# Selective scan: the two halves of the weighted states are added on GpSimd ahead of its decay factors, and TensorE sums eight states in place of sixteen

## The reference, cut to what matters

```python
z = h @ in_w.T
gate = jax.nn.silu(h @ gate_w.T)
A = -jnp.exp(A_log)
Bi = z @ Bp_w.T
Ci = z @ Cp_w.T
dt = jax.nn.softplus(z @ dt_w.T + dt_b)
A_bar = 1.0 + dt[..., None] * A
def step(state, inp):
    a_bar, dtz_t, b_t, c_t = inp
    state = a_bar * state + dtz_t[:, :, None] * b_t[:, None, :]
    y = jnp.sum(state * c_t[:, None, :], axis=-1)    # over 16 states
    return (state, y)
...
y = jnp.swapaxes(ys, 0, 1) * gate
return y @ out_w.T
```

## Time and profile before

| | us |
|---|---|
| median of three runs | 2525.13 |
| the profiled execution | 2515.18 |
| its span, first to last instruction | 2513.4 |
| busy in the span: PE / DVE / ACT / POOL | 2233.5 / 1666.2 / 1317.3 / 809.1 |
| the scan, about | 824 to 953 of the span |
| two stretches of 13.40 us inside it (878.0 to 904.8), DVE busy in each | 11.99 |
| the same, PE and POOL busy in each | 13.40 and 5.96 |

### The profile page before, as it was taken

How to read it: one execution, slowest core, us unless ns; L and a number is a source line. 1 busy time by engine, 2 the same in 40 slices (tenths; PEclk the granted TensorE clock), 3 DMA queues, 4 the chain that set the end, 5 groups by cost and what they waited for, 6 DMA issues and landing times. The chain is left out here.

```text
span 2513.4 us, 48220 instructions
## 1 busy us (share of the span) xinstructions
PE 2233.5 (89%) x17198; PEld 1778.7 (71%) x17200; DVE 1666.2 (66%) x3232; ACT 1317.3 (52%) x3079; POOL 809.1 (32%) x1019
## 2 busy tenths in 40 slices
PE   6979798999698898989999879999689998899775
PEld 5857687887476796778888468888556566788652
DVE  5767635774575686764777456666567575888758
ACT  4558636664576653533666343333475464445345
POOL 4646502332354442100333112222110110544365
PEclk9989989999899899979999989999899999999888
DMA  3000081115200000060211420000200002777711
GB/s 112 2 1 2 32 331 64 51 51 175 92 2 2 22 2 1 2 259 20 101 51 51 175 103 1 2 1 1 101 1 1 1 1 77 227 212 212 231 28 34
DMA packets 102932, 178.35 MB, mean 71 GB/s; under 512 B 59687, under 2 KB 71591, under 8 KB 97578
## 3 DMA queue, kind: packets, MB, share of 16 engines
q1 hardware_dynamic: 85514, 135.93, 16.3%
q0 software_dynamic: 9792, 28.85, 3.6%
q10 hardware_dynamic: 7392, 10.49, 1.1%
HBM read 112.44 MB, written 62.78 MB: 70 GB/s over the span
## 5 line engine op out<-in xcount | busy, mean ns | idle before, releaser
L2289 POOL TENSOR_TENSOR l2a_Pn<-l2a_Pn,l2a_rden 128x1024 f32<-128x1024 f32 x32 | 60.1, 1899 | 295.2 <-DVE l2a_rden L2531 295.2
L1617 ACT ACTIVATE l0f_w_parts<-l0f_W 128x512 fp32r (+1 forms) x117 | 90.4, 775 | 68.2 <-PE l0f_psG L1422 50.3
L1768 DVE TENSOR_TENSOR l0f_w_parts<-l0f_W,l0f_w_parts 128x512 fp32r<-128x512 f32 (+1 forms) x117 | 99.2, 867 | 37.7 <-ACT l0f_w_parts L1617 37.6
L1617 ACT ACTIVATE l1f_w_parts<-l1f_W 128x512 fp32r (+1 forms) x117 | 90.4, 774 | 63.0 <-PE l1f_psG L1422 50.2
L4054 POOL TENSOR_TENSOR l3x_Pn<-l3x_Pn,l3x_fac 128x616 f32<-128x616 f32 (+2 forms) x96 | 70.4, 763 | 149.8 <-DVE l3x_fac L4133 140.4
L1768 DVE TENSOR_TENSOR l1f_w_parts<-l1f_W,l1f_w_parts 128x512 fp32r<-128x512 f32 (+1 forms) x117 | 99.2, 867 | 12.6 <-ACT l1f_w_parts L1617 12.2
L1475 PE MATMUL l1f_psY<-l1f_W,l1f_XT_hT 128*128 (+1 forms) x440 | 104.2, 380 | 0.8 <-ACT l1f_XT_hT L1597 0.8
L883 ACT ACTIVATE l1a_att_Pn<-l1a_att_psS,l1a_att_nmx 128x128 f32<-128x128 f32 x256 | 92.1, 422 | 1.7 <-DVE l1a_att_nmx L1002 1.7
L883 ACT ACTIVATE l0x_Pn<-l0x_psS,l0x_nmx 128x128 f32<-128x128 f32 x256 | 92.1, 422 | 0.9 <-DVE l0x_nmx L1002 0.9
L706 POOL TENSOR_TENSOR l1a_att_Pn<-l1a_att_Pn,l1a_att_rden 128x512 f32<-128x512 f32 x64 | 66.6, 1041 | 73.3 <-DVE l1a_att_rden L1009 73.3
L1475 PEld LDWEIGHTS l1f_psY<-l1f_W,l1f_XT_hT 128*128 128x128 f32 x440 | 80.3, 190 | 10.8 <-issue 1.0
(11 more groups left out here) (860 smaller groups left out, 7504.4 us busy)
## 6 DMA issues: line engine op xcount, KB each, us to landing
relative_rows<-l3x_ext SPq DMA_DIRECT2D x32, 516.0 KB, 5.8
l1f_W<-in_l1f_w SPq DMA_DIRECT2D x9, 1536.0 KB, 20.6
l0f_W<-in_l0f_w SPq DMA_DIRECT2D x8, 1536.0 KB, 26.1
cumulative_rows<-l3x_cum SPq DMA_DIRECT2D x32, 384.0 KB, 3.4
l3x_K<-keys SPq DMA_DIRECT2D x16, 512.0 KB, 5.5
l3x_rel<-relative_rows SPq DMA_DIRECT2D x32, 231.0 KB, 4.3
values<-l1f_W SPq DMA_DIRECT2D x11, 512.0 KB, 4.4
l3x_V<-values SPq DMA_DIRECT2D x16, 308.0 KB
```

Of the source, the lines that this page charges most:

```text
L1617: nc.scalar.activation(w_high[i], W[:, bass.ds(act_offsets[k] + o, m)], ACT.Copy).then_inc(high_ready, 1)
L1768: nc.vector.tensor_tensor(w_low[i], W[:, bass.ds(dve_offsets[k] + o, m)], w_high[i], ALU.subtract).then_inc(low_ready, 1)
L2289: nc.gpsimd.tensor_tensor(part, part, rden[b % 2][:, 8 * u:8 * u + 8].unsqueeze(2).to_broadcast([P, 8, P]), ALU.mult)\
```

## The change

GpSimd gets a new step `add_halves(p)`: u[:, 0:1024] = u[:, 0:1024] + u[:, 1024:2048], one 128x1024 f32 addition in SBUF. It waits for the second `weigh` of pair p and stands in GpSimd's list behind L1980 of pair p+1 and ahead of the decay factors of pair p+1 (for p = 7, at the list's end). `sum_states(p)` waits for it and takes eight blocks where it took sixteen.

```diff
+    halved = R.sem("states_halved")
...
+        def add_halves(p):
+            pool.wait_ge(weighted, 2 * p + 2)
+            nc.gpsimd.tensor_tensor(half(u[p % 2], 0), half(u[p % 2], 0), half(u[p % 2], 1), ALU.add).then_inc(halved, 1)
+
         for p in range(NP2):
             pool.wait_ge(xn_ready, p + 1)
             xp = G.x[:, 2 * p * D:2 * (p + 1) * D]
             nc.gpsimd.tensor_tensor(xp, xp, saved[:, 2 * p * D:2 * (p + 1) * D], ALU.add).then_inc(summed, 1)
+            if p:
+                add_halves(p - 1)
             pool.wait_ge(dt_ready, p + 1)
...
+        add_halves(NP2 - 1)
...
         def sum_states(p):
             past(pe, x_ready, 2 * p)
-            for s in range(ST):
-                if s % HS == 0:
-                    pe.wait_ge(weighted, 2 * p + s // HS + 1)
-                ins = nc.tensor.matmul(psS, G.ident[:, :], u[p % 2][:, s * P:(s + 1) * P], start=(s == 0), stop=(s == ST - 1))
+            pe.wait_ge(halved, p + 1)
+            for s in range(HS):
+                ins = nc.tensor.matmul(psS, G.ident[:, :], u[p % 2][:, s * P:(s + 1) * P], start=(s == 0), stop=(s == HS - 1))
             ins.then_inc(sum_done, 1)
```

## The result

| | before | after |
|---|---|---|
| median of six runs, us | 2524.16 (2518.23 to 2528.76) | 2534.87 (2530.99 to 2538.71) |
| ratio of the runs, 95% interval | 1 | 1.0047 (1.0034 to 1.0060) |
| span of the profiled execution, us | 2513.4 | 2533.6 |
| the scan: first `gates` reciprocal to the next sublayer's first VectorE instruction on x (L539), us | 118.73 | 127.96 |
| the rest of the span, us | 2394.7 | 2405.6 |

The change makes the kernel slower by 0.47% (0.34 to 0.60); the medians lie 10.7 us apart. The scan accounts for 9.2 us. The spans lie 20.2 us apart, and the other 11 us of that are in the main scatter of single traces. The scan begins 6.7 us later in the trace of the changed kernel (842.0 against 835.3 us), so that much was lost in sublayers that run before any edited instruction.

The account below looks back on a forecast made before the run. No engine fills the kernel alone; in the scan TensorE and VectorE are in turn on the path, GpSimd off it. 9.0 + 0.9 + 0.4 - 0.5 = +9.8 us on 2525.13 gives 2534.9 us, range 2519 to 2546.

Parts of the forecast that it names:

- pairs 2 to 6: Steady pairs of the scan: each 1.8 us longer, five times 1.8, +9.0 us.
- the end: Last pair's sum: starts later with half the blocks, 2.7 to 3.1 us long; `gate_y` released 0.5 us earlier (0 to -1.3).
- The addition: GpSimd's new 128x1024 f32 addition per pair: takes 2.36 us, bounds 1.90 to 2.52.
- Step 2: VectorE's dtz, with two SBUF inputs, stands behind GpSimd's addition, making VectorE about 2.08 us late per pair.
- Step 3: After the addition, dtz was waiting first and goes ahead of GpSimd's decay pass, 0.29 us.
- rival B: GpSimd keeps its turn, dtz also stands behind the first decay pass, 1.99 us more; +17.1, 2542 us; chance 0.10.
- Step 4: VectorE through `drive` keeps its pace; `gate_y` loses its 1.34 us wait; first scan ready 0.74 us later.
- Step 5: GpSimd's addition to x starts 0.1 us before the first scan is ready; the scan stands another 1.04 us.
- The sum does not wait for GpSimd: B products occupy TensorE until about 892.75, past the addition's end at 892.25; the sum runs 892.75 to 894.6.
- Rival A: The two engines don't hamper each other enough to matter; the wait goes: -10.4, 2514.7 us; chance 0.12.
- Rival C: TensorE's clock falls in its longer gaps; two such stretches cost 0.9 per pair, 5 to 6 us, 2540 us; chance 0.06.
- Rival D: Only dtz collides and the addition to x slips past the scans: +4.5, 2529.6 us; chance 0.12.

Follow-up runs that it names:

- e4: Changed kernel with GpSimd's addition cut from 1024 to 128 columns and seven of the second eight states left out of the sum; one run, 2516.98 us.
- e6: Changed kernel with a 128x2048 memset in place of GpSimd's addition, second eight states left out of the sum; one run, 2518.58 us.
- e9: Changed kernel with VectorE's dtz moved from behind dt to just before `drive`; one run, 2524.15 us.
- e2: Changed kernel with the addition written to a tile nobody reads and all sixteen blocks summed; ratio to before 1.0039 (1.0019 to 1.0058).
- e1: Kernel before with TensorE summing only states 0 to 7 and no addition on GpSimd; ratio to before 0.9956 (0.9939 to 0.9972).
- e10: The changed kernel once more, unaltered, for a second trace; ratio to before 1.0037 (1.0023 to 1.0052).
- e3: Changed kernel with GpSimd's addition to x waiting until both scans of the pair before are done; ratio to before 1.0014 (1.0003 to 1.0025).
- e5: Changed kernel with the next pair's dt and dtz taken between the two `weigh`s, before the event releasing the addition; ratio to before 1.0017 (1.0005 to 1.0030).
- e8: Changed kernel with e3's and e5's edits, ScalarE making decay factors 8 to 11, its copies first, VectorE adding the last halves; ratio to before 0.9962 (0.9947 to 0.9978).

## Why the prediction was right

The mechanism and the sign are right, and the exact agreement of the time (2534.9 forecast, 2534.87 measured) is luck. The forecast added 9.8 us to a median of three runs, 2525.13; of six runs it was 2524.16, and the medians then differed by 10.7. The 9.8 itself is a sum in which steps too high and too low nearly cancel, and the measured difference holds 1.5 us that lie outside the scan or are scatter. By where the scans of each pair end, worked out from their starts and durations, against the same points of before:

| step | forecast, us | trace, us |
|---|---|---|
| pair 1 | +0.4 | +0.6 |
| pairs 2 to 6 | 5 x 1.8 = +9.0 | 5 x 1.55 = +7.7 |
| pair 7 | +0.9 | +0.8 |
| the end | -0.5 | +0.1 |
| scan stage | +9.8 | +9.2 |

- **The addition, 2.36 us**: 2358 ns median. Right, from the row of equal form.
- **Step 2, dtz late by 2.08**: 2352 instead of 292 ns, 2.06. Right, and e4 (445 ns behind 455), e6 (0.29 beside a memset) and e9 (1.90 behind another instruction) show that it is this mechanism.
- **Step 3, dtz ahead of the decay pass**: right; rival B needed 4.3.
- **Step 4, the wait of 1.34 gone**: right. VectorE gained 0.09 us more, since without the pause `gate_y` starts 0.09 us before `drive` has ended.
- **Step 5, the scan behind the addition to x**: right in place and order; sized at 1.04, measured 0.92. Its start leads the scan's issue by 0.22, not 0.1 us. With the 0.09 above and 0.02 at dtz that is the way from the 1.78 worked out for this order to 1.55. The prediction took a scan alone as 2.23 us, half of a merged row of 4.46; the two overlap there, and each alone has 2.28 and 2.27.
- **The sum does not wait for GpSimd**: its consequence right, its account incomplete. TensorE stood 1.35 us for `add_y`; it ended in time all the same. In e2, with the whole sum, this wait becomes 0.70 us on the path.
- **The end**: wrong in sign, and outside the 0 to -1.3 given for it. I let eight blocks take 2.7 to 3.1 us, after 3.40 us at the lower clock in the trace of before. TensorE was now without work for 5.99 us, the clock was low for 6.8 us, and all eight blocks fell into that and took 3.71.
- **Rival A** is refuted by e1 as well: without the new addition the pair is 12.91, not 12.09. **Rival C** is in the trace, but costs nothing: the clock was at 0.50 from 869.8 to 873.2 and from 944.9 to 948.3, and yet the pairs with these stretches lose 1.54 and 0.78 us against before, as in the second trace (1.54 and 0.77 in e10), where the clock stayed up from 852.7 to 958.4 with the same pauses of TensorE. One such stretch in a pair is covered by the microsecond that the sum has in hand, as the prediction had it for one; two in a pair did not occur. The windows row below is the first stretch, in the changed kernel's trace. **Rival D**: e3 makes its case on purpose, 14.05 us per pair against the 14.2 worked out for it.

```profile
869.80:873.10 3.30, 3.30 (x18) 3.30 (x17) 3.27 (x4) 2.58 (x9) 2.74 (x2) 0.50 0.00 0
```

The forecast hung on an overlap that in a steady pair of before never happens. It could be priced because the first pair, out of step with the rest, had all three collisions in it.

## What to carry to other kernels

Before work goes from TensorE to GpSimd, mark in the timeline which VectorE instructions have both inputs in SBUF, and ask for each of GpSimd's which of them it will meet; the price is not its own duration on an idle engine but what is left of it when they meet. Look for the spans in the trace that are longer than their group's median: they show such meetings where the steady loop hides them. The cure is to let the event that starts GpSimd come after the short two-input instruction, and to lay GpSimd's reads beside VectorE's work on PSUM. Each of these alone was a small edit and took 0.9 us off a pair (e3, e5), and left the kernel slower than before. Only together, with GpSimd's decay passes halved and the copies moved, did they beat it (e8, 12.54 us per pair against 14.98 with the same addition in it). No run tells what the two do together without the rest.

## What the runs showed of the hardware

- The exclusion works by instruction and by turn: dtz, 0.29 us alone, took 0.45, 1.90 and 2.35 us behind GpSimd instructions of 0.46, 1.88 and 2.37 us (e4, e9, the changed kernel). Each time it ended 0.15 us after the GpSimd instruction's recorded end, so with its own 0.29 us it began shortly before that end. The profile shows no wait for it, only a longer span.
- A memset on GpSimd excluded nothing (dtz 0.29 us beside 1.80 us of it). The Trainium skill, "SBUF — State Buffer", section "Who interferes with whom", says that a VectorE instruction with two SBUF inputs contends with a GpSimd one that reads SBUF and not with one that only writes; these runs agree on both halves, the second by the memset alone.
- A VectorE instruction with one input in PSUM was never held up (in none of the thirteen traces does one of the sixteen `drive` or sixteen `weigh` instructions take over 1.23 us): the two of a pair together, `drive` took 2.32 us with GpSimd reading beside it (e8), `weigh` 2.32 beside the addition to x (e3).
- The part of the program outside the scan, the same instructions in all kernels, took from 2394.7 to 2408.7 us in thirteen traces. The mean granted clock goes with a part of it: of 26 timed runs of the kernel before the fastest, 2513.47 us, had 0.950 and the slowest, 2531.40, had 0.940. It is not all: e5 and e9, both with 0.944, have rests of 2408.7 and 2394.8 us. The cause of the scatter stays open.
